# A vision transformer block on one core: weighting behind the transposes, last rows on two engines, turns among the weight transposes, experts' weights rounded in pieces

## The reference

```
h = tokens(x)      # 16x16 patches, layernorm, 768->192 projection, layernorm, + positions; 2 class rows in front: 198 rows of 192
h = h + attention(layernorm(h))   # 12 heads of 64; scores and outputs also get relative-position tables (30 rows, vertical and horizontal)
h = h + experts(layernorm(h))     # shared MLP 192->192->192 with relu^2, plus the best 2 of 8 such experts per token, weighted by sigmoid scores
```

## Time and profile before

| | us |
|---|---|
| median of 3 runs | 4549.45 |
| lowest, highest | 4533.93, 4564.05 |
| the profiled execution | 4544.49 |
| its span, first to last instruction | 4542.5 |
| PE busy in the span | 4128.4 |

### The profile page before, as it was taken

How to read it: one execution, slowest core, us unless ns; L and a number is a source line. 1 busy time by engine, 2 the same in 40 slices (tenths; PEclk the granted TensorE clock), 3 DMA queues, 4 the chain that set the end, 5 groups by cost and what they waited for, 6 DMA issues and landing times. The chain is left out here.

```text
span 4542.5 us, 84795 instructions
## 1 busy us (share of the span) xinstructions
PE 4128.4 (91%) x28203; PEld 4011.3 (88%) x28203; DVE 2946.3 (65%) x7462; ACT 2474.0 (54%) x6670; POOL 1266.1 (28%) x1418
## 2 busy tenths in 40 slices
PE   4984799899899999989989999998999699999999
PEld 4984599899899989989989998998998599999999
DVE  4674466666666656666666666666666477777777
ACT  2552666556666656656655665666664244444443
POOL 1233122222222222213212222222222144444443
PEclk8997899999999999999999999999999799999999
DMA  8542000000000000000000000000000122222222
GB/s 181 134 108 66 2 1 1 1 23 1 1 23 1 1 2 23 1 1 23 1 1 11 13 1 2 23 1 1 12 1 1 45 85 87 92 96 94 87 87 84
DMA packets 88737, 161.69 MB, mean 36 GB/s; under 512 B 5579, under 2 KB 75810, under 8 KB 84704
## 3 DMA queue, kind: packets, MB, share of 16 engines
q1 hardware_dynamic: 84896, 152.66, 11.9%
q0 software_dynamic: 944, 2.42, 0.3%
q10 hardware_dynamic: 2560, 2.36, 0.2%
HBM read 127.82 MB, written 29.60 MB: 35 GB/s over the span
## 5 line engine op out<-in xcount | busy, mean ns | idle before, releaser
L602 POOL TENSOR_TENSOR att_prob<-att_prob,att_total 99x396 f32<-99x396 f32 x768 | 650.7, 847 | 2353.0 <-DVE att_total L848 2353.0
L678 ACT ACTIVATE att_probT<-att_t 99x396 f32<-99x396 f32 x768 | 385.1, 501 | 1044.3 <-PE att_t L994 1041.1
L856 DVE TENSOR_REDUCE att_npeak<-att_s 99x2 f32<-99x396 f32 x768 | 436.7, 569 | 746.6 <-PE att_s L1028 742.9
L1011 PE MATMUL att_o<-att_probT,att_vx 99*96 99x198 f32 (+1 forms) x3072 | 675.4, 343 | 27.8 <-DVE att_rx L841 26.8
L1028 PE MATMUL att_s<-att_kx,att_qx 96*99 96x198 f32 (+1 forms) x3072 | 664.6, 339 | 6.1 <-issue 5.7
L690 ACT ACTIVATE att_prob<-att_s,att_npeak 99x198 f32<-99x198 f32 x1536 | 636.7, 424 | 17.5 <-DVE att_npeak L856 17.0
L1195 POOL TENSOR_TENSOR ffn_hidden<-ffn_relu 128x384 f32<-128x384 f32 x462 | 417.7, 909 | 510.9 <-ACT ffn_relu L1224 508.6
L1011 PEld LDWEIGHTS att_o<-att_probT,att_vx 99*96 99x96 f32 (+1 forms) x3072 | 505.0, 182 | 58.6 <-issue 38.0
L1028 PEld LDWEIGHTS att_s<-att_kx,att_qx 96*99 96x99 f32 (+1 forms) x3072 | 522.7, 170 | 23.5 <-issue 7.0
L1224 ACT ACTIVATE ffn_relu<-ffn_h 128x384 f32<-128x384 f32 x462 | 226.1, 490 | 496.7 <-PE ffn_h L1433 495.8
L1445 PE MATMUL ffn_y<-ffn_down,ffn_hidden 128*128 128x192 f32 x2772 | 487.1, 326 | 0.0
(11 more groups left out here) (204 smaller groups left out, 8126.8 us busy)
## 6 DMA issues: line engine op xcount, KB each, us to landing
ffn_gates<-gate_rows SPq DMA_DIRECT2D x66, 768.0 KB, 5.1
tok_pixels<-in_x SPq DMA_DIRECT2D x24, 1568.0 KB
ffn_hid<-hidden SPq DMA_DIRECT2D x35, 288.0 KB, 3.0
att_xres<-hidden SPq DMA_DIRECT2D x8, 1188.0 KB
hidden<-att_xres SPq DMA_DIRECT2D x8, 1188.0 KB
ffn_acc<-hidden SPq DMA_DIRECT2D x33, 288.0 KB, 2.9
out_hidden<-ffn_acc SPq DMA_DIRECT2D x33, 288.0 KB, 2.4
hidden<-tok_rows SPq DMA_DIRECT2D x8, 1176.0 KB
```

The lines of the kernel that those rows point to most:

```text
L602: nc.gpsimd.tensor_tensor(prob[:, i % 2, :, :], prob[:, i % 2, :, :], view(total[:, i % 2, :], [[1, 2], [0, NTOK]]), ALU.mult).then_inc(pr ...
L678: nc.scalar.activation(probT[:, i % 2, :], t_bank[0:HALF, 0:2 * NTOK], ACT.Copy).then_inc(probT_made, 1)
L856: nc.vector.tensor_reduce(npeak[:, i % 2, :], s_bank[i % 2][0:HALF, 0:2 * NTOK].rearrange("p (h k) -> p h k", h=2), AX.X, ALU.max, negate= ...
L1011: ins = nc.tensor.matmul(o_bank[0:M, 0:NTOK], vx[:, 2 * b + k, p % 2, v0:v0 + M], probT[:, j % 2, k * NTOK:(k + 1) * NTOK], start=(k == 0) ...
```

## The change

Four things change, in different places.

1. **Attention's steps.** PE weights item n-3 right behind the transposes of item n-2, ahead of the step's jobs. DVE inverts the sums first, and copies the output of item n-3 (not n-4) out, in the step in which it is made.
2. **Tokens.** The first group's pixels get a semaphore per channel, and DVE's first statistics go channel by channel. In the last group POOL scales and shifts only the first 6 of 14 columns; DVE does the other 8 itself, and the store is two DMAs. POOL's loop is written out.
3. **Start of attention.** The weight transposes use four banks (s_bank, t_bank, o_bank), begin with the output projection as soon as its weights and the last two qkv blocks are in, and the eight opening turns stand among the others: 8 transposes, then a turn and two transposes, eight times. The tables come after them; clearing att_kx and copying the one-hot rows into it go from DVE to POOL. The second load of residual rows moves behind SP's table loads.
4. **Start of the experts.** The up weights come in five pieces (shared and router, then two experts each), ACT writes the high parts, DVE the low parts, and PE waits for each piece alone.

```diff
@@ tokens, DVE: first statistics
-                dve.wait_ge(pixels_in[0], 16 * CH)
-                for wv in range(SIDE):
-                    ins = statistics1(0, wv)
+                for c in range(CH):
+                    dve.wait_ge(channel_in[c], 16)
+                    for wv in range(SIDE):
+                        ins = nc.vector.bn_stats(stat1[:, wv, c, :], view(pixels[:, 0, c, :], [[IMG, PATCH], [1, PATCH]], wv * PATCH))
...
@@ tokens, DVE: end of the last group (POOLED = 6)
+                        if wv == (SIDE if more else POOLED) - 1:
                             ins.then_inc(rows_normed, 1)
+                    if not more:
+                        ins.then_inc(last_normed, 1)
+                        dve.wait_ge(last_normed, 1)
+                        rest = SIDE - POOLED
+                        nc.vector.tensor_tensor(rows[:, s, POOLED:, :], rows[:, s, POOLED:, :], view(g2[:, :], [[0, rest], [1, DIM]]),
+                                                ALU.mult).then_inc(last_scaled, 1)
+                        dve.wait_ge(last_scaled, 1)
+                        dve.wait_ge(posb_made, 1)
+                        nc.vector.tensor_tensor(rows[:, s, POOLED:, :], rows[:, s, POOLED:, :], posb[:, POOLED:, :], ALU.add
+                                                ).then_inc(last_made, 1)
...
@@ attention, order of the weights' transposes
-            return [("qkv", t) for t in range(QROWS // 128)] + [("proj", p) for p in range(PAIRS)]
+            return [("proj", p) for p in range(PAIRS)] + [("qkv", t) for t in [*range(RAW, QROWS // 128), *range(RAW)]]
...
@@ attention, POOL
+                nc.gpsimd.memset(kx[:], 0.0).then_inc(keys_cleared, 1)
                 nc.gpsimd.memset(qx[:], 0.0)
-                pool.wait_ge(prep_full, len(prep_jobs()))
+                pool.wait_ge(prep_full, PAIRS)
                 nc.gpsimd.memset(rx[:], 0.0).then_inc(zeroed, 1)
+                pool.wait_ge(zeroed, 1)
+                pool.wait_ge(keys_cleared, 1)
+                for s in range(2):
+                    for lo, head in ((64, 0), (32, 1)):
+                        pool.wait_ge(keys_made, 2 * s + head)
+                        nc.gpsimd.tensor_copy(view(kx[lo:lo + 32, s, head, :], [[NTOK, GB], [1, NTOK]]),
+                                              view(onehot[:, :], [[0, GB], [1, NTOK]])).then_inc(keys_made, 1)
...
@@ attention, DVE: a step
-                    j = i - 4
+                    j = i - 3
-                    dve.wait_ge(outs, n - 4 + 1)
+                    dve.wait_ge(outs, n - 3 + 1)
...
-                        if v != "first" or i >= 4:
-                            put_out(n, i)
                         if v != "first" or i >= 1:
                             inverted_sums(n, i)
+                        if v != "first" or i >= 3:
+                            put_out(n, i)
...
@@ attention, DVE (ACT and PE alike): the opening (EARLY = 8)
+                for n in range(EARLY):
+                    prep(n)
                 begin_turns(0, 0, st)
-                for j in opening:
+                for j in range(TURN):
+                    job(0, -1, 1, "opening", *opening[j])
+                    for n in (EARLY + 2 * j, EARLY + 2 * j + 1):
+                        prep(n)
...
@@ attention, PE: a step
                         if v != "first" or i >= 2:
                             turn_probs(n, i)
+                        if v != "first" or i >= 3:
+                            weigh(n, i, base, v)
                         for j in spreads[v][i]:
                             job(base, g, v, *j)
-                        if v != "first" or i >= 3:
-                            weigh(n, i, base, v)
...
@@ experts, ACT
+                def weights_high(i):
+                    lo, hi = PIECES[i]
+                    act.wait_ge(piece_in[i], 32)
+                    if i == 0:
+                        act.wait_ge(router_in, 32)
+                    nc.scalar.activation(w0h[:, lo:hi], raw0[:, lo:hi], ACT.Copy)
+                    for at in (0, C1):
+                        ins = nc.scalar.activation(w1h[at:at + C1, lo:hi], raw1[:, lo:hi], ACT.Copy)
+                    ins.then_inc(piece_high, 1)
...
@@ experts, DVE
+                low(0, 0)
+                for i, (lo, hi) in enumerate(PIECES):
+                    dve.wait_ge(piece_high, i + 1)
+                    nc.vector.tensor_tensor(w0l[:, lo:hi], raw0[:, lo:hi], w0h[:, lo:hi].bitcast(fp32), ALU.subtract)
...
                 dve.wait_ge(w_in, 16 * WEIGHTS)
-                dve.wait_ge(router_in, 32)
-                nc.vector.tensor_copy(w0h[:, :], raw0[:, :])
...
-                low(0, 0)
...
@@ experts, PE
-                pe.wait_ge(w_made, 3)
                 for n in range(HT):
+                    if n == 0 or (n >= SHARED and CHUNKS[n] % 3 == 0):
+                        pe.wait_ge(piece_low, 1 if n == 0 else 2 + CHUNKS[n] // 3)
```

More of the change, by code:

```diff
@@ L89, in tokens_stage @@
     SLOTS = 3
+    POOLED = 6
     with ExitStack() as ctx:
@@ L895, in _, with prep @@
             def _(pe):
-                pe.wait_ge(onehot_made, 9)
-                pe.wait_ge(raw_in, 16 * 4)
-                for n, (kind, t) in enumerate(prep_jobs()):
-                    if n >= 2:
-                        pe.wait_ge(prep_free[n % 2], n // 2)
-                    bank = p_bank[n % 2]
+                pe.wait_ge(onehot_made, 2)
+                def prep(n):
+                    kind, t = prep_jobs()[n]
+                    if n == 0:
+                        pe.wait_ge(raw_in[0], 48)
+                    elif kind == "qkv" and t in (0, RAW // 2):
+                        pe.wait_ge(raw_in[2 if t else 1], 16)
+                    if n >= 4:
+                        pe.wait_ge(prep_free[n % 4], n // 4)
+                    bank = prep_bank[n % 4]
                     if kind == "qkv":
@@ L1112, in experts_stage @@
         AHEAD = 3
-        WEIGHTS = 8
+        WEIGHTS = 4
+        PIECES = [(EXPERTS * DIM, HID + EXPERTS)] + [(2 * i * DIM, 2 * (i + 1) * DIM) for i in range(EXPERTS // 2)]
         with nc.Block() as block:
@@ L1237, in _ @@
                 high(0, 0)
+                for i in range(len(PIECES)):
+                    weights_high(i)
                 act.wait_ge(odds_cleared, 1)
```

196 lines of the change are left out of this document (110 added, 86 removed).

## The result

The changed kernel took 4433.64 us (median of 4 runs, 4426.74 to 4439.13) against 4545.62 for the kernel before on the same chip (4 runs). The ratio is 0.9749, with a 95% interval of 0.9713 to 0.9786: 112 us, or 2.5%, faster. The forecast was 4411, with a range of 4365 to 4472.

What follows compares the result with a forecast made beforehand. PE in attention, two thirds of the time, was taken as the bound. Attention's waits 84, clock 20, tokens 6, attention's start 11 and experts' start 13 sum to 134 us off 4544.5: 4411 us, range 4365 to 4472.

Steps and rivals of the forecast that it cites:

- the likeliest case: Whole kernel: the summed gains hold, 134 us, mostly from attention's order of weighting; given 71%.
- `last` 8: Attention's steps: this job's 48 PE waits, 82.7 us, shrink by 0.36 us in 41 and 0.68 in 7; gain 19.5 us.
- `last` 0: Attention's steps: this job's 40 waits, 34.2 us, go as the output is copied a step earlier; 28 us taken.
- The weighting's bank: Attention's steps: the weighting's 53 waits for its bank, 26.8 us, go except in steps with no job; gain 24 us.
- The turns: Attention, projections behind the turns: moved weighting covers part of their waits, 14 x 0.68 + 3.3; gain 12.8 us.
- The clock: Attention: fewer 1.2 GHz stretches after shorter waits, 19 us plus 1 from the last group's steps without jobs; gain 20 us.
- Tokens: End of the tokens stage: POOL begins earlier with 6 of 14 columns, DVE does the rest; gain 6 us.
- lower case of 3.3: End of tokens: gain 3.3 us if DVE's last normalisations are held up as well, against 5.7 otherwise.
- Start of attention: From the residual rows' arrival to the first projection: 39 us in place of 49.9; gain 11 us, bounds 0 and 17.
- Start of the experts: Router's first scores come 14 us sooner, 13 taken; 8 if all weight pieces arrive late.
- the waits re-form: Rival, 14%: attention's front-of-step weighting waits for ACT; 44 us there, no clock gain, 25 at borders; 4476 us.
- The slower case: Rival, 3%: attention's weighting waits for ACT's copy of turned probabilities in 192 steps; 0.95 us each gives 4590.

Runs made afterwards that it cites:

- the last three runs: On the changed kernel: `last` 8 in the next step, 4329.44 us; that plus POOL's clears and copies ahead of its DMA issues, 4321.56; both plus turns earlier, 4292.52.

## Why the prediction was right, and where its steps failed

The total was inside its range, and the likeliest case held: attention's steps carry three quarters of the gain (84.5 of 112 us by the medians). The steps one by one:

- **`last` 8: failed.** Forecast 19.5 us, and the waits fell by 1.8 in all. The failed step is "the copies begin at about 1004.49, 0.54 late": it took the start of DVE's peak behind the scores as given and looked only at what the copies wait for. The peak's start was itself set by DVE's adds, which had lost the weighting as cover in front of the scores. The run with short adds shows it: there the copies do wait for the weighting, and the waits are 1.23 us where the prediction's sum gives 1.52 less 0.36.
- **`last` 0: the mechanism right, the size in part by luck.** 33.2 us of the wait went, 15.0 came back as a wait for ACT in the second and fourth pairs, at the transposes and not at the weighting. The forecast was 28, in terms of waits, and by waits it is 18. By the lengths of the steps it is 26: 1.5 us in each of 23 steps with a wait of 1.23, 0.6 in each of 16 with one of 0.31, less 1.15 in each of the 16 with the wait for ACT. The 8 between stand in no wait, and the forecast did not reckon with such time.
- **The weighting's bank: right**, 24 forecast, 25.7 by the waits.
- **The turns: failed**, 12.8 forecast, 1.1 lost. The first projection's wait got longer (4.1 to 4.4), the second's shorter (about 2.5 to 1.9), the third's longer (about 0.5 to 1.0). The failed step is that the weighting "now lies in front of the wait and covers part of it". For the first of the three the traces show why: between the projection ahead and the one that waits, PE's list has the scores, the transposes, the weighting and the turn in both kernels, in another order. The chain that it waits for starts with ACT's copy of the projection ahead (L652, now L686), and from there to the projection it took 6.50 us before (1205.55 to 1212.06 in the second group) and 6.49 now (1171.43 to 1177.92), in each of the seven groups within 0.02. So the weighting covered that wait before as well. For the other two it is argued from the same order.
- **The clock: right in sum, by other members.** 20 forecast, 22.2 measured. But the forecast had 19 of it in the loop and 1 in the last group's end. It was 10.2 in the loop (33 stretches in place of 37: the three behind `last` 0 and the two behind the scores went, behind the turns there are 14 in both, and behind `last` 8, where the forecast took 8 away, 19 for 18) and 12.0 in the last 100 us, where 41 us of slow time became 17.
- **Not in the sum: 22.0 us.** It went by the printed waits. Matmuls that follow each other overlap in the profile, so some 0.2 us of most waits looked at here stand as busy time of the one ahead. By the lengths of the steps the 22 to 24 us lie at the bank (about 14) and at `last` 0 (about 11), less about 4 behind the new waits for ACT. For the bank the run with early copies shows it; for the rest it is read from the steps alone.
- **Tokens: right** (6.5 against 6), in two halves of which it had one. The normalisations were held by 4.7 us, so the last operation ended 3.6 sooner, which is the forecast's lower case of 3.3; and attention's load was issued 5.9 us behind that operation (413.02 to 418.93) and no longer 8.8 (417.72 to 426.52), behind a store of 8 columns in place of 14. With 5 and 9 columns stored together at the end it was 7.5 (the run with POOL behind all normalisations); that the size of the last store is the cause is argued.
- **Start of attention: mis-sized**, 7.2 against 11, and of the 7.2 only 3.7 lie behind the arrival, where the 11 were forecast; the arrival's 3.5 stood in its bounds and not in its sum. The term that failed is the hold of DVE by POOL. It was named for the one-hot copies, "can hold each up", and given no price; the clears, which held longest, were not named. It cost 10.8 us (12.62 in place of 1.83). With POOL's work out of the way the first projection came 37.6 us behind the arrival, near the 39 of the forecast.
- **Start of the experts: right**, 14.1 against 13. ACT's roundings took 7.0 us and not 5.5, but its first relu came 23.8 us behind the last residual add, where the forecast had it (3609 on the scale of before).

So 32 us were forecast at `last` 8 and the turns that did not come, and 22 came that were not forecast. That the total was near is in part luck. Of the rivals, "the waits re-form" was half there (16.5 us for ACT), but the clock's gain was not lost with it. (That rival's sum has 25 us for the borders, the forecast's 30, without a reason; it changes nothing here.) The slower case needs the weighting to wait for ACT in 192 steps; L1060 has no such row. The kernel with late copies shows that another loss was nearer: the weighting may only move together with the copy. The copy needs no such partner, as the run with early copies shows.

## What to carry to other kernels

When an instruction moves in a ring of steps, follow the cover that it gave to both sides: what lay behind it in the old place loses what the new place gains, and where the other engine works without a pause, neither place matters. Then move the consumer a step on instead: the dependent job put in the next step won 104 us, where moving the work around it won nothing at that place. Ask also which of two moves made together brings the gain: here the earlier copy alone gave 71.7 us, and the other move alone lost a quarter. And a list of waits is no full bill: a wait that is not printed was worth 0.24 us in each of 32 steps, and only the lengths of the steps showed it.

## What the hardware showed

- **The lower clock after waits goes with their length.** In attention of ten of the kernels (before, after, and all but the last three runs) without its last 100 us, a stretch at 1.2 GHz began around the end of a wait (1.2 us ahead to 1.5 behind) at none of 277 waits under 0.6 us, at 28 of 332 between 0.6 and 1.35, at 83 of 268 between 1.35 and 1.7, at 33 of 95 between 1.7 and 2, and at 52 of 89 between 2 and 3. These are counts, of waits in different places; for one place the short adds show it. In the changed kernel 13 of the 31 waits of `last` 8 between 1.35 and 1.7 us had one; with the adds cut none of the 38 between 1.0 and 1.35 had. Most were 3.4 us long and so cost 1.7. A wait shortened by 0.4 us was thus worth more than its 0.4.
- **Equal code, unequal clock.** In the kernels whose attention waits alike (the changed one and three others: idle 162 to 166 us, work 2765 to 2767) the slow time of one execution was 143 to 164 us, so one profile is sure to about 10 us.
- **POOL's writes alone hold DVE.** A memset, which reads nothing, held a normalisation for 7.9 us in place of 0.46 (1.83 for four). The statistics and the low parts read from PSUM, beside the same clears, were not held.
